# Graph-network layers on one core: an if and else on each third's kept tile, and kept tiles loaded without bounds instructions

## The reference

```python
def _rgat(x, src, dst, etype, W, Q, K, b, heads, out_ch, n):
    xw = jnp.einsum('ni,rio->rno', x, W)
    out_i = xw[etype, dst]
    out_j = xw[etype, src]
    alpha = jax.nn.leaky_relu(out_i @ Q + out_j @ K, SLOPE)
    alpha = _segment_softmax(alpha, dst, n)
    msg = (out_j.reshape(-1, heads, out_ch) * alpha[..., None]).reshape(-1, heads * out_ch)
    return jax.ops.segment_sum(msg, dst, num_segments=n) + b
```

## Time and profile before

| | |
|---|---|
| median of 3 runs | 5981.1 us (5980.46 to 5985.14) |
| the profiled execution's own time | 5983.0 us |
| its span | 5981.2 us |
| busy in the span: PE, DVE, ACT, POOL | 67%, 50%, 33%, 61% |
| mean granted TensorE clock | 0.77 of full speed |
| attentions in the span, from the first to the last of their instructions | 1490 to 2256, 2515 to 3284, 3434 to 4146 us |
| filter stage, mean over edges | 4324 to 5122, 5268 to 5958 us |

### The profile page before, as it was taken

How to read it: one execution, slowest core, us unless ns; L and a number is a source line. 1 busy time by engine, 2 the same in 40 slices (tenths; PEclk the granted TensorE clock), 3 DMA queues, 4 the chain that set the end, 5 groups by cost and what they waited for, 6 DMA issues and landing times. The chain is left out here.

```text
span 5981.2 us, 75465 instructions
## 1 busy us (share of the span) xinstructions
PE 4017.4 (67%) x17120; PEld 2952.3 (49%) x17121; DVE 3013.1 (50%) x6900; ACT 1976.6 (33%) x4675; POOL 3626.0 (61%) x2851
## 2 busy tenths in 40 slices
PE   5599932497677778777777634444499999745553
PEld 5488821253455555355555523333367767533332
DVE  6566636621555552255555434444467777533334
ACT  0022200000555551066555112211088888300000
POOL 0244412076877753587774688885677777478884
PEclk6699965698788888888888755555799999865655
DMA  0000001333665543466553323332344444243332
GB/s 7 23 11 12 11 21 31 99 83 63 178 167 159 155 113 91 106 175 171 153 157 91 78 72 84 81 83 78 81 115 119 120 120 119 74 105 84 84 85 73
DMA packets 510833, 558.34 MB, mean 93 GB/s; under 512 B 302100, under 2 KB 394239, under 8 KB 510285
## 3 DMA queue, kind: packets, MB, share of 16 engines
q0 software_dynamic: 349600, 362.07, 24.5%
q1 hardware_dynamic: 157688, 186.99, 10.8%
q10 hardware_dynamic: 3250, 6.40, 0.4%
HBM read 460.15 MB, written 92.22 MB: 92 GB/s over the span
## 5 line engine op out<-in xcount | busy, mean ns | idle before, releaser
L1259 POOL DMA_INDIRECT sum_gx_sb<-scratch_xw,keep_k_row_step_sb x1272 | 1605.0, 1262 | 462.0 <-issue 354.3
L1372 PE MATMUL sum_a_ps<-sum_gx_sb,sum_sel_sb 125*125 125x258 f32 (+1 forms) x4320 | 1211.9, 444 | 542.7 <-ACT sum_gx_sb L1308 220.4
L1372 PEld LDWEIGHTS sum_a_ps<-sum_gx_sb,sum_sel_sb 125*125 125x125 f32 x4320 | 935.4, 242 | 733.5 <-issue 514.1
L1308 ACT ACTIVATE sum_gx_sb<-sum_gx_sb,sum_wt_sb 125x129 f32<-125x129 f32 x3312 | 982.0, 390 | 550.8 <-DVE sum_wt_sb L1501 531.2
L2497 POOL DMA_INDIRECT filter_gx_sb<-scratch_h,keep_k_src_step_sb x424 | 584.4, 1378 | 194.3 <-issue 97.8
L1168 POOL DMA_INDIRECT scratch_grouped<-keep_k_value_sb,keep_k_place_sb x400 | 483.0, 1207 | 269.5 <-issue 134.6
L2968 POOL DMA_INDIRECT source_gx_sb<-scratch_h,source_grouped_sb x424 | 523.1, 1234 | 140.0 <-issue 121.0
L2980 PE MATMUL source_s_ps<-source_gx_sb,source_sel_sb 125*125 125x257 f32 x848 | 364.9, 605 | 310.1 <-DMA source_gx_sb<-scratch_h,source_grouped_sb 310.1
L2980 PEld LDWEIGHTS source_s_ps<-source_gx_sb,source_sel_sb 125*125 125x125 f32 x848 | 242.4, 299 | 432.9 <-issue 153.2
L2554 PE MATMUL filter_ps<-filter_m_sb,filter_h_sb 128*125 128x256 f32 x1696 | 386.7, 381 | 1.6 <-DVE filter_h_sb L2624 1.5
L3007 DVE TENSOR_TENSOR keep_agg_sb<-source_s_ps,keep_agg_sb 125x257 f32 x424 | 181.0, 427 | 382.3 <-PE source_s_ps L2980 370.9
(11 more groups left out here) (515 smaller groups left out, 6869.6 us busy)
## 6 DMA issues: line engine op xcount, KB each, us to landing
scratch_hots<-sum_cuts_sb SPq DMA_DIRECT2D x108, 244.1 KB
filter_sel_sb<-scratch_hots SPq DMA_DIRECT2D x106, 244.1 KB
sum_gx_sb<-scratch_xw,keep_k_row_step_sb POOLq DMA_INDIRECT x1272
scratch_xw<-gate_xsb_sb SPq DMA_DIRECT2D x50, 253.9 KB
scratch_xw<-attend_xsb_sb SPq DMA_DIRECT2D x25, 507.8 KB
filter_ea_sb<-in_ea_t SPq DMA_DIRECT2D x424, 24.4 KB
filter_gx_sb<-scratch_h,keep_k_src_step_sb POOLq DMA_INDIRECT x424
source_gx_sb<-scratch_h,source_grouped_sb POOLq DMA_INDIRECT x424
```

The lines of the kernel that those rows point to most:

```text
L1259: nc.gpsimd.indirect_dma_start(out=gx[:, q, j, :], out_offset=None, in_=table, in_offset=bass.IndirectOffsetOnAxis(ap=keep["row_step"][:, ...
L1308: last = nc.scalar.activation(here, here, ACT.Copy, scale=wt[q][:, h, j:j + 1])
L1372: last = mm(psa[b][0:P, half, 0:BF], sel[:, 0, p, j, :], gx[:, q, at, half * BF:(half + 1) * BF], **flags)
```

## The change

`node_tiles` and `part_tiles` load their registers without the bounds instructions, and the second of the two tests on a part becomes the else of the first, on PE and on DVE. What is loaded, summed and added stays, and so do all semaphores.

```diff
 def node_tiles(nc, keep, first, count):
-    _, tiles = nc.values_load_multi_w_load_instructions(keep["nk"][0:1, bass.ds(first, count)], engines=(mybir.EngineType.DVE,),
-                                                        min_val=0, max_val=NT - 1)
+    _, tiles = nc.values_load_multi_w_load_instructions(
+        keep["nk"][0:1, bass.ds(first, count)], engines=(mybir.EngineType.DVE,), min_val=0, max_val=NT - 1,
+        skip_runtime_bounds_check_because="node tiles of steps are made on chip within 0 and NT - 1")
     return tiles
...
     _, values = nc.values_load_multi_w_load_instructions(
-        keep["part"][:].rearrange("o s p -> o (s p)")[:, bass.ds(s * parts, parts)], engines=(engine,), min_val=0, max_val=NT)
+        keep["part"][:].rearrange("o s p -> o (s p)")[:, bass.ds(s * parts, parts)], engines=(engine,), min_val=0, max_val=NT,
+        skip_runtime_bounds_check_because="parts are made on chip as tile numbers below NT, or NT")
     return values
...
                     with pe.If(tiles[p] < NT):
                         sums(s, q, p, True)
-                    with pe.If(tiles[p] > NT - 1):
+                    with pe.Else():
                         sums(s, q, p, False)
...
-                with dve.If(firsts[p] > NT - 1):
+                with dve.Else():
                     tiles = node_tiles(nc, keep, n, HF)
```

## The result

| | before | changed |
|---|---|---|
| median, lowest and highest run | 5980.8 us (5980.5 to 5985.1) | 5910.1 us (5903.5 to 5911.2) |
| ratio, 95% interval | | 0.9875 (0.986 to 0.9889) |
| profiled execution, span | 5981.2 us | 5901.7 us |
| three attentions, from the first `sum` instruction to the next stage | 768.8, 770.2, 716.5 us | 732.1, 739.6, 708.2 us |
| filter stage, from its first to its last instruction | 798.4 us | 796.5 us |

The kernel is 71 us faster by the medians, 75 by the ratio. The forecast was 49 us, 5934 us, and the range ended at 5908: by the ratio the kernel stands at 5906, just under it, by its own median at 5910. By the prediction's own signs, two attentions "shorter by over 30" us speak against it: they are 36.7 and 30.6 us shorter.

What follows compares the result with a forecast made beforehand. PE and DVE were taken to bound the late stretches of the first two attentions, gathers the early ones and most of the third. 2 x 22.3 + 4.7 = 49.3 us off 5983.0 gave 5934 us, range 5908 to 5961.

Steps and rivals of the forecast that it cites:

- shorter by over 30: Sign that the prediction is wrong: the first two attentions shorter by over 30 us, where some 22 us each was forecast.
- What bounds each stretch: First two attentions: gathers lead early, PE and DVE lead blocks 17 to 35; gathers lead the third nearly throughout.
- Checks in mixed parts: DVE's four node-tile checks in parts sharing no tile: 13 x 1.08 = 14.0 us for each of the first two attentions.
- The stretches led by gathers: Early blocks of the first two attentions: removed checks shorten only POOL's stalls, 3.3 us for each attention.
- PE's three checks: Before a block's first matmul, partly hidden behind DVE's drain: 2.6 us for each of the first two attentions.
- in full: Rival: PE's checks at block starts count fully, 0.8 us in 38 blocks, 30 instead of 5 us, 5909; chance 0.11.
- DVE's three checks: In part 1, exposed only where part 0 is mixed: 4 x 0.43 = 1.7 us in each late stretch.
- The second test: Lost DVE comparison in mixed parts, 13 x 0.05 = 0.7 us per attention; the plain jump in even parts changes nothing.
- Third attention: Only its last three blocks gain: 2.3 us from two mixed parts, 2.4 from DVE's part 1 checks, 4.7 us.
- Filter stage: Its 16 mixed quads lose four DVE checks each, covered by PE's matmuls: 0, up to 1 us.
- The gathers take over: Rival: half the gain in the first two attentions becomes waits for landings, 22 us lost, 5956; chance 0.14.
- The stalled jump: Rival: the jump over the else body at even parts' ends stalls instruction fetch, 81 us, 6015; chance 0.04.

Runs made afterwards that it cites:

- the profiles named above: With checks: kernel before, and only the else added (5982.0 us); without: the change, its repeat (5911.1 us), and only the bounds instructions removed (5917.1 us).
- the pair of runs: Constant bfloat16 matmuls added in PE's pauses of mixed parts, to the kernel before (5955.0 us) and to the changed kernel (5886.6 us).

## Why the prediction was right or wrong

The steps that failed are two terms of the sum: the mixed parts were priced too low, and the gathers were held at their duration. Averages over the profiles named above (two with checks, three without) against the terms; block 17's mixed part is counted in the early stretch here, and the terms are split to match.

| us | forecast | measured |
|---|---|---|
| first two attentions, blocks 1 to 17 | 8.8 | 15.3 |
| blocks 18 to 35 | 35.8 | 43.4 |
| their first block and end | 0 | 0.9 |
| third attention | 4.7 | 6.8 |
| filter stage | 0 | 1.4 |
| all other stages | 0 | 4.0 |
| sum | 49.3 | 71.8 |

- *What bounds each stretch*: right. The late stretches gave most, PE and DVE lead them, and POOL's stalls there fell by 16.8 and 17.7 us (20 predicted).
- *Checks in mixed parts, 13 x 1.08*: the right mechanism, mis-sized. The idle time before the first add fell by 1.21 us in the part shown, 1.20 on average in the early mixed parts. From the operation ahead to the end of the last add the late mixed parts lost 1.5 us on average (5.8 to 4.3), where the terms (checks, second test, DVE's own checks) gave 1.26. Over 24 parts that explains 6 of the 7.6 us that the late stretches gave beyond the forecast. The step that failed took the stretch between the load's end and the last check, in place of the idle time as a whole; read to the last digit that stretch is 1.11 us, not 1.08.
- *The stretches led by gathers, 3.3*: this step failed. "A check taken away shortens nothing but a stall of POOL" held the gathers at their duration. In the averages of the table POOL's idle time fell by 5.7 us in the two early stretches (8.8 forecast, with block 17), and its gathers took 9.5 us less, as fewer of them collided with DVE's operations. That it came out so is a matter of timing that no term of the sum could have named.
- *PE's three checks, 2.6 for each attention*: right (the earlier trace rows moved by 0.79, not, and PE's part load alone gave 8 us, 2 to 13, where 5 was predicted and 30 by "in full"). That rival's time, 5909, came out for other reasons, so its nearness to the measured 5910 is chance.
- *DVE's three checks, 4 x 0.43*: right. Where part 0 is mixed, the idle time before the first add fell by 1.7 us in the late stretches, elsewhere by 1.2.
- *The second test, 0.7 and nothing for the jump*: right, 0.9998. PE's plain jump takes 0.17 us where the taken comparison took 0.21; on DVE it is 0.05 against 0.06. The Trainium skill's rule (Advanced Engine Details and Errata, Control Flow Timing) would have made it 5 us; the run's interval reaches from 6.6 us faster to 4 slower, and its median is within 2 us of no change, so these 5 us are neither shown nor excluded.
- *Third attention, 4.7*: 6.8 on average. Behind the last gather 3.9 us went, as the term had it; ahead of it POOL's idle time stayed as it was and the gathers took 3.3 us less, which the term held at nothing.
- *Filter stage, 0*: right within the scatter. It gave 1.4 us, and kernels that keep the node checks differ by as much among themselves.
- *The gathers take over*: began, 8.8 and 1.4 us of new waits for landings, not 22.
- *No term for TensorE's clock*: a real gap, since the clock is worth 24 to 30 us in this kernel. Of the gain it is no part that the pair of runs could show, and 13 us at most by the estimate above.
- The last 4.0 us lie in stages with unchanged code, where single profiles scatter by as much (the gate stage stands at 340.4 to 345.4 us in the kernels run). They stay open.

These are the two test lines after, over the whole trace, each with 324 tests and, under the same name, the 276 plain jumps of the even parts:

```profile
L1401 PEldq COMPARE_BRANCH  x600: 65/169/328, 1535.2 to 4062.4; - x150
```

```profile
L1549 DVEq COMPARE_BRANCH  x600: 43/47/80, 1538.1 to 4064.3; - x150
```

The stalled jump, the slower rival, would have shown here as more than 0.5 us a part.

## What to carry to other kernels

Instructions of a sequencer between a register load and its use count in full where an engine has nothing else to do; take their cost from the whole idle time in front of the operation they hold, not from their own rows, and remove them even where the engine's mean load is 50%. A small error of price repeats: 0.24 us in each of 24 parts was 6 us of a 71 us result. And a stretch "led by the gathers" is not rigid: look at what makes single gathers long before putting its term at zero.

## What the runs showed of the hardware that was not expected

- A gather was held by VectorE with no semaphore between the two: one that starts in the first 0.3 us of L1508 or L1516, VectorE operations of 0.66 to 0.70 us on two SBUF operands, took 1.58 us on average in place of 1.21 and ended 1.08 to 1.09 us behind the operation in 72 of 80 cases. None took over 1.4 us when it started in an add that reads PSUM.
- Sixteen useless bfloat16 matmuls in each mixed part made the kernel 24 to 30 us faster. Ten of them, 1.26 us, were enough in the part shown for the next four float32 matmuls to take 1.13 instead of 2.08 us, though PE then stood idle for 2.31 us in between. Twenty-eight in place of sixteen raised the granted clock of the late stretches from 0.90 to 0.92 and gave nothing (5889.3 against 5886.6 us).
- A bounds instruction pair costs a sequencer 0.28 us from pair to pair (on DVE 0.18 to 0.19 for the first, 0.02 for the assert, the rest between them; on PE 0.15 and 0.02). A load of four node tiles took 0.36 us (median), one of three numbers of `keep["part"]` 0.77 to 0.78, up to 1.11 on PE. It isn't the table: `quad_tiles` (L2444) loads four numbers from it in 0.33 to 0.35 us.
